# Weights of a quantised MoE block laid out with the contracted dimension on the partitions, and the engine orders laid anew

## The chip, the core and the metric

The kernel runs on one core of a Trainium2 chip. The core has a matrix engine (TensorE, PE in the rows; PEld is its weight load), a vector engine (VectorE, DVE), a scalar engine (ScalarE, ACT), GpSimd (POOL) and a queue engine (SyncE, SP). Each engine works through its own list in order and waits on semaphores for the others. The metric is the device time of one execution in microseconds (us); lower is better.

## What is computed

Four batches of 256 tokens, 256 wide, pass two stages. The first is a small gated MLP whose two linears are quantised to 8 bits per row after a per-column smoothing. The second routes every token to one of 8 experts (at most 128 tokens per expert) and runs the expert's two-layer MLP on it.

```python
def _smooth_quant_linear(x, w):
    amax_x = jnp.max(jnp.abs(x), axis=0)
    amax_w = jnp.max(jnp.abs(w), axis=0)
    s = jnp.sqrt(jnp.maximum(amax_x, EPS) / jnp.maximum(amax_w, EPS))
    xs = x / s
    ws = w * s
    # per-row scales, rounding to 8-bit integers, then
    return x_q @ w_q.T * x_scale * w_scale.T

def _expert_forward(xe, guw, dw):          # first stage, per batch
    h = _smooth_quant_linear(xe, guw)      # guw = fside_BxS2xS2_0[b]: 256 x 256
    gate, up = jnp.split(h, 2, axis=-1)
    return _smooth_quant_linear(jax.nn.silu(gate) * up, dw)   # dw = ctx_1024[b]: 256 x 128
...
x = x + jnp.tanh(g_xattn[0]) * first_stage(_layernorm(x))
x = x + jnp.tanh(g_ffn[0]) * top1_experts(_layernorm(x), w_gate, w1, w2)   # 8 experts, 256 -> 1024 -> 256, gelu
```

The maxima over the rows of a weight (axis 0) are what the smoothing needs; with the contracted dimension on the partitions they are maxima along a row of the memory.

## The kernel before

Everything is held in SBUF; the order of every engine is written out by hand as a list of calls, one list per engine, with batches 0 to 3 (`b`) interleaved. A semaphore ties each call to its producers.

**First stage, per batch b.** SP loads x and the gate/up weight `cw` (L230 to L243), then the router weight `wg`, the down weight `dw`, the two gate scalars, a clear of the scratch rows in HBM, and the expert weights (L244 to L278). VectorE takes mean and variance (`stats1`), GpSimd the reciprocal deviation (`rstd1`), ScalarE the normalised rows (`norm1`; GpSimd for b = 3). TensorE turns the normalised rows (`turn1`) and the weight (`turn1w`) into one PSUM pair `bk[b]`; VectorE takes both maxima (`amax1w`, `amax1`) and their ratio, GpSimd the square root (`root_1`), ScalarE scales both (`scale1`; VectorE for the weight of b = 3), TensorE turns them back (`turn2`), VectorE finds the row scales (`scales1`), ScalarE multiplies and rounds (`quantise1`), GpSimd finishes the rounding (`round1`), TensorE turns the integers (`turn3`) and multiplies (`product1`). `rows1` puts the token scales in a row and the router's logits beside it in `bk[b]`; ScalarE moves that row (`move_row1`). Then `gate_up` on VectorE, `silu` on ScalarE, `act_product` on GpSimd.

The down linear repeats this: `down_turn` turns `dw` on TensorE, `down_amax` takes its maxima on VectorE (and, in its last instruction, scales the logits into `lx`), `amax2`, `root_2`, `scale2`, `turn4`, `scales2`, `quantise2`, `round2`, `turn5`, `move2`, `product2`. `fill` calls are matmuls whose result is not used.

**Routing.** `choose` (VectorE) picks the expert of each token, `expert_out` adds the first stage's result to x, `positions` (TensorE) counts places, `place` and `slot_onehot` make slot numbers and one-hot rows, `square2` and `rstd2` the second norm. `dispatch` (TensorE) gathers the rows of experts 0 and 1 by a product with the one-hot rows, eight matmuls per batch, accumulating over all four batches; `scatter` (GpSimd) writes all rows to the scratch in HBM, two indirect transfers per batch, from which experts 2 to 7 are read back (L281 to L284) once all eight have landed.

**Experts.** For e = 0 to 7: `hidden` (w1), gelu on ScalarE twice (high part and full), `split_high`/`split_low` cut w2 in two parts, `hidden_low` the hidden layer, `expert_out` on TensorE. VectorE enters this stage only after the last scatter has been issued (`scatters_begun`, L932).

## Time and profile before

| | us |
|---|---|
| median of 3 runs | 116.8 (116.26 to 116.91) |
| the profiled execution's own time | 117.76 |
| its span, first to last instruction | 116.0 |
| TensorE busy / VectorE / ScalarE / GpSimd | 98.6 / 86.7 / 72.3 / 56.0 |
| granted TensorE clock, mean | 0.995 |

The span begins with the first instruction and ends with the last; the execution's own time has 1.76 us around it. A row of a timeline gives start, duration, engine, line, operation, tiles and how many instructions were merged; in brackets stands how long the engine had been idle and who ended that. The word `issue` means a wait that the profile ties to nothing.

### The profile page before, as it was taken

To read this page: it belongs to the slowest core of one execution; us is meant where nothing else is said; L and a number is where in the kernel's file an instruction comes from. 1 tells how busy PE (TensorE), PEld (TensorE's weight loads), DVE (VectorE), ACT (ScalarE), POOL (GpSimd) and SP (SyncE) were. 2 spreads that over 40 slices of the span, in tenths; PEclk is the share of its full clock that TensorE was granted. 3 is DMA by queue.
4 is the path that set the end of the run, shared out by engine and by line. 5 is a ranking of instruction groups with operands and counts; after the bars stand their busy time and mean duration, and the time that the engine had idled before them with its cause. 6 is when DMAs were issued, how large, how long until landed. Compare 5 with 4: busy or idle time off the path is not lost.

```text
span 116.0 us, 2229 instructions
## 1 busy us (share of the span) xinstructions
PE 98.6 (85%) x741; PEld 84.4 (73%) x741; DVE 86.7 (75%) x231; ACT 72.3 (62%) x154; POOL 56.0 (48%) x119
## 2 busy tenths in 40 slices
PE   0948868997986898996889999999999999999930
PEld 0227546996845667874689989899999989899820
DVE  6646897999997889682318698999898696939450
ACT  4073579798797899966018564998573739376000
POOL 7855598787969849878670000426030303011041
PEclk9999999999999999999999999999999999999998
DMA  3899998999990942409932999989898860101011
GB/s 108 255 353 291 240 172 291 323 363 353 378 328 26 292 149 94 160 25 237 346 103 66 292 398 353 309 214 408 303 330 280 298 236 10 45 0 51 0 45 45
DMA packets 16218, 24.86 MB, mean 214 GB/s; under 512 B 1368, under 2 KB 13913, under 8 KB 15184
## 3 DMA queue, kind: packets, MB, share of 16 engines
q1 hardware_dynamic: 15440, 22.65, 62.1%
q0 software_dynamic: 768, 2.08, 4.8%
q8 instruction: 6, 0.10, 0.3%
q14 instruction: 4, 0.03, 0.1%
HBM read 20.50 MB, written 4.28 MB: 214 GB/s over the span
## 4 chain that ended last, share of the span: by engine, by line
PE 50%; POOL 16%; DVE 14%; issue 6%; DMA 6%; SPq 2%; ACT 2%; POOLq 1%
PE bk L1182 25%; PE bk L1194 11%; PE bk L1196 6%; DMA cw<-in_ctx_gu 6%; POOL slot_rows L426 4%; POOL row L412 2%; DVE am L740 2%; PE bk L1168 2%; POOL sc L370 2%; DVE am L786 2%; PE bk L1155 2%; PE bk L1208 2%; PE bk L1019 1%; SPq L231 1%; DVE am L721 1%
## 5 line engine op out<-in xcount | busy, mean ns | idle before, releaser
L494 POOL DMA_INDIRECT out<-scrow,gr x8 | 9.5, 1182 | 43.1 <-DVE scrow L961 41.7
L1182 PE MATMUL bk<-rows_w,w_sb 128*128 128x128 f32 x192 | 23.0, 275 | 0.5 <-ACT rows_w L583 0.5
L1182 PEld LDWEIGHTS bk<-rows_w,w_sb 128*128 128x128 f32 x192 | 22.2, 192 | 0.8 <-ACT rows_w L583 0.7
L1194 PE MATMUL bk<-w2p,hh 128*128 128x512 f32 x56 | 20.3, 403 | 0.0
L862 DVE TENSOR_TENSOR w2p<-w_sb,w2p 128x1024 fp32r<-128x1024 f32 x12 | 14.1, 1217 | 3.8 <-POOL begun L482 2.7
L1196 PE MATMUL bk<-w2p,hl 128*128 128x256 f32 x56 | 15.6, 278 | 0.0
L597 ACT ACTIVATE w2p<-w_sb 128x1024 fp32r<-128x1024 f32 x12 | 12.0, 1054 | 5.3 <-PE bk L1196 5.3
L661 ACT ACTIVATE hh<-bk 128x512 fp32r<-128x512 f32 x16 | 9.5, 595 | 4.7 <-PE bk L1182 4.7
L1194 PEld LDWEIGHTS bk<-w2p,hh 128*128 128x128 f32 x56 | 10.5, 188 | 2.1
L1196 PEld LDWEIGHTS bk<-w2p,hl 128*128 128x128 f32 x56 | 10.5, 188 | 0.0
L874 DVE TENSOR_TENSOR hl<-wide_a,hh 128x512 fp32r<-128x512 f32 x16 | 10.4, 683 | 0.0
L1013 PE MATMUL bk<-identb,upper 128*128 128x512 bf16 x25 | 7.8, 438 | 3.0 <-POOL upper L308 3.0
L426 POOL DMA_INDIRECT slot_rows<-row,slot x8 | 8.7, 1090 | 2.9 <-issue 2.9
L663 ACT ACTIVATE wide_a<-bk 128x512 f32<-128x512 f32 x16 | 9.6, 598 | 0.0
L1155 PE MATMUL bk<-row,wide_b 128*128 128x258 f32 x32 | 7.9, 391 | 1.8 <-POOL row L415 1.8
L1155 PEld LDWEIGHTS bk<-row,wide_b 128*128 128x128 f32 x32 | 5.8, 190 | 2.9 <-issue 2.2
L531 ACT ACTIVATE wide_a<-bk,sc 128x256 f32<-128x256 f32 x14 | 5.4, 482 | 2.3 <-POOL sc L370 2.3
L513 ACT ACTIVATE rows_w<-x,sh,rs 128x256 f32<-128x256 f32 x6 | 3.3, 593 | 5.3 <-POOL sh L333 5.3
L540 ACT ACTIVATE wide_b<-bk,q1r 128x256 f32<-128x256 f32 x16 | 6.4, 494 | 0.0
L1013 PEld LDWEIGHTS bk<-identb,upper 128*128 128x128 bf16 x25 | 2.5, 107 | 5.0 <-POOL upper L308 3.0
L1048 PE MATMUL bk<-ident,wide_a 128*128 128x128 f32 x32 | 4.5, 281 | 1.0 <-ACT wide_a L531 0.9
L1048 PEld LDWEIGHTS bk<-ident,wide_a 128*128 128x128 f32 x32 | 3.4, 140 | 2.5 <-ACT wide_a L531 2.4
(164 smaller groups left out, 229.9 us busy)
## 6 DMA issues: line engine op xcount, KB each, us to landing
w_sb<-in_w SPq DMA_DIRECT2D x12, 1024.0 KB, 7.4
slot_rows<-empty SPq DMA_DIRECT2D x1, 1068.0 KB, 9.9
x<-in_x SPq DMA_DIRECT2D x4, 256.0 KB, 4.3
cw<-in_ctx_gu SPq DMA_DIRECT2D x4, 256.0 KB, 6.3
cw<-in_w SPq DMA_DIRECT2D x1, 1024.0 KB, 7.1
out<-row SPq DMA_DIRECT2D x4, 256.0 KB, 2.6
x<-in_w SPq DMA_DIRECT2D x1, 1024.0 KB, 5.8
wide_a<-in_w SPq DMA_DIRECT2D x1, 1024.0 KB, 6.7
```

The lines of the kernel that those rows point to most:

```text
L426: nc.gpsimd.indirect_dma_start(scratch, bass.IndirectOffsetOnAxis(ap=slot[:, b, j:j + 1], axis=0), row[:, b, j, 0:ROW], None, bounds_check ...
L494: nc.gpsimd.indirect_dma_start(out_rows, bass.IndirectOffsetOnAxis(ap=gr[:, e, TOKEN:TOKEN + 1].bitcast(I32), axis=0), yo[:, e % 2, :], No ...
L597: last = nc.scalar.activation(w2p[:, e % 2, n:n + NF // 2, 0], w2v[:, n:n + NF // 2], ACT.Copy)
L661: nc.scalar.activation(hh[:, e % 2, part].rearrange("p n c -> p (n c)"), HB[e % 2][:, m, :], ACT.Gelu_apprx_tanh).then_inc(hhigh_ready, 1)
L663: nc.scalar.activation(hs[:, e % 2, part].rearrange("p n c -> p (n c)"), HB[e % 2][:, m, :], ACT.Gelu_apprx_tanh).then_inc(gelu_ready, 1)
L862: last = nc.vector.tensor_tensor(w2p[:, e % 2, part, 1], w2v[:, part], w2p[:, e % 2, part, 0].bitcast(F32), ALU.subtract)
L874: nc.vector.tensor_tensor(hl[:, e % 2, part], hs[:, e % 2, part], hh[:, e % 2, part].bitcast(F32), ALU.subtract).then_inc(hlow_ready, 1)
L1013: nc.tensor.matmul(bk[b][:, a, :], upper[:], identb[:].unsqueeze(1).to_broadcast([P, 4, P]), start=True, stop=True)
L1155: ins = nc.tensor.matmul(XD[e], hot[:, b, j, e * C:(e + 1) * C], row[:, b, j, 0:RSTD + 1], start=(b == 0 and j == 0), stop=(b == B - 1 and ...
L1182: ins = nc.tensor.matmul(HB[e % 2][:, m, n * C:(n + 1) * C], wv[:, k, o:o + P], xgT[:, e % B, k], start=(k == 0), stop=(k == K - 1))
L1194: nc.tensor.matmul(YB[e % 2], hh[:, e % 2, n], w2p[:, e % 2, n].rearrange("p a d -> p (a d)"), start=(n == 0), stop=False)
L1196: ins = nc.tensor.matmul(YB[e % 2][:, 0:D], hl[:, e % 2, n], w2p[:, e % 2, n, 0], start=False, stop=(n == NF - 1))
```

## The change

`kernel()` on the host reorders four inputs before they are handed over, so that each load is one contiguous row per partition: `cw` becomes [128, K, 256] with the contracted dimension on the partitions, `dw` [128, B, 256], `wg` [128, K, 8], and w2 [E, 128, 8, 256]. What follows from it:

- `turn1w` and `down_turn` are gone from TensorE. `amax1w` reads `cw` in SBUF and also takes the floor and the reciprocal there; `amax1` keeps one reduction and one combined instruction. `down_amax` is gone: one call `down_maxima` reduces all four batches in one reduction over 1024 columns, a floor and a reciprocal; its last instruction lives on as `lx_scale(b)`.
- ScalarE's `scale1(b, 1)` and the second half of `scale2` read SBUF where they read PSUM. `scale1(3, 1)` moves from VectorE to ScalarE, `move_row1` from ScalarE to VectorE.
- The loads of `wg` and of the two gate scalars are issued by ScalarE ahead of its first table load, no longer by SP. SP's order is x, cw alternating for b = 0 to 3, then `dw`. SP waits for the last `scale1` of the weights, not for `turn1`, before it loads w2 of expert 3 over `cw`.
- `slot_onehot(3)` is cut in two instructions, and `dispatch(3)` waits for each apart.
- The lists of all four compute engines are written anew.

```diff
             def load_cw(b):
-                sp.dma_start(cw[:, b], ctx_in[b].rearrange("(j p) d -> p j d", p=P)).then_inc(cw_here[b], 16)
-            load_x(0)
-            load_x(1)
-            load_cw(0)
-            load_x(2)
-            load_cw(1)
...
-            sp.dma_start(dw[:], down_in.rearrange("b (k p) i -> p b k i", p=P)).then_inc(dw_here, 16)
...
+                sp.dma_start(cw[:, b], ctx_in[b]).then_inc(cw_here[b], 16)
+
+            for b in range(B):
+                load_x(b)
+                load_cw(b)
+            sp.dma_start(dw[:], down_in).then_inc(dw_here, 16)
...
+            act.dma_start(wg[:], w_gate).then_inc(wg_here, 16)
+            act.dma_start(gates[:, 0:1], g_xattn.partition_broadcast(P)).then_inc(small_here, 16)
+            act.dma_start(gates[:, 1:2], g_ffn.partition_broadcast(P)).then_inc(small_here, 16)
...
             def amax1w(b):
-                dve.wait_ge(t1w_ready, b + 1)
-                mark(nc.vector.tensor_reduce(am1[:, b, K:2 * K], bk[b][:, 1].rearrange("p (k t) -> p k t", k=K),
-                                             AX, ALU.max, apply_absolute_value=True))
+                dve.wait_ge(cw_here[b], 16)
+                link(nc.vector.tensor_reduce(am1[:, b, K:2 * K], cw[:, b], AX, ALU.max, apply_absolute_value=True))
+                link(nc.vector.tensor_scalar(am1[:, b, K:2 * K], am1[:, b, K:2 * K], EPS, None, ALU.max))
+                inverse_written[b] = mark(nc.vector.reciprocal(rw1[:, b], am1[:, b, K:2 * K]))
...
+            def move_row1(b):
+                dve.wait_ge(row1_ready, b + 1)
+                nc.vector.tensor_copy(xrow[:, b], bk[b][:, 1, 0:T]).then_inc(row1_moved, 1)
...
+            def down_maxima():
+                dve.wait_ge(dw_here, 16)
+                link(nc.vector.tensor_reduce(amd[:], dw[:], AX, ALU.max, apply_absolute_value=True))
+                link(nc.vector.tensor_scalar(amd[:], amd[:], EPS, None, ALU.max))
+                down_inverse[0] = mark(nc.vector.reciprocal(rwd[:], amd[:]))
...
@@ VectorE's list, the routing end
-            scales2(2)
-            choose(0)
-            expert_out(0)
-            scales2(3)
...
+            scales2(2)
+            choose(0)
+            scales2(3)
+            expert_out(0)
```

**VectorE around the first `gate_up`.** In the fences bk0 to bk3 are the PSUM pairs of the four batches; the reduction of am2 from bk3 is `scales1(3)`, wide_a from bk0 is `gate_up(0)`. Before:

```order
L745 RECIPROCAL q1r<-q1s 128x4
L732 TENSOR_SCALAR wide_a<-bk3,sc1 128x256 x2
L752 SCALAR_TENSOR_TENSOR wide_a<-bk0,q1s,scrow 128x256 x2
L761 TENSOR_REDUCE amd<-bk0 128x1
L762 TENSOR_SCALAR amd<-amd 128x1
L763 RECIPROCAL rwd<-amd 128x1
L765 TENSOR_TENSOR lx<-bk0,irs 128x2x8
L740 TENSOR_REDUCE am2<-bk3 128x2 x2
```

The same place now:

```order
L724 RECIPROCAL q1r<-q1s 128x4
L729 COPY scrow<-bk0 128x256
L747 TENSOR_REDUCE amd<-dw 128x4
L748 TENSOR_SCALAR amd<-amd 128x4
L749 RECIPROCAL rwd<-amd 128x4
L736 SCALAR_TENSOR_TENSOR wide_a<-bk0,q1s,scrow 128x256 x2
L719 TENSOR_REDUCE am2<-bk3 128x2 x2
```

The copy of the row and the pass over all down weights stand ahead of `gate_up(0)`; the scaling of the last weight and batch 0's own down maxima are gone.

**GpSimd at the end of the routing.** Three instructions (ve2, row, row) are one `rstd2`, two of the DMA rows one `scatter`. Before, from `rstd2(2)` on:

```order
L406 TENSOR_SCALAR ve2<-ve2 128x2
L412 TENSOR_TENSOR row<-ve2,mhalf 128x2
L415 TENSOR_TENSOR row<-row 128x2
L426 DMA slot_rows<-row,slot 1024x267 x2
L406 TENSOR_SCALAR ve2<-ve2 128x2
L412 TENSOR_TENSOR row<-ve2,mhalf 128x2
L415 TENSOR_TENSOR row<-row 128x2
L426 DMA slot_rows<-row,slot 1024x267 x4
L482 MEMSET begun 128x1
```

Now, from `rstd2(2)` on:

```order
L396 TENSOR_SCALAR ve2<-ve2 128x2
L402 TENSOR_TENSOR row<-ve2,mhalf 128x2
L405 TENSOR_TENSOR row<-row 128x2
L396 TENSOR_SCALAR ve2<-ve2 128x2
L402 TENSOR_TENSOR row<-ve2,mhalf 128x2
L405 TENSOR_TENSOR row<-row 128x2
L416 DMA slot_rows<-row,slot 1024x267 x6
L472 MEMSET begun 128x1
```

`rstd2(3)` no longer stands behind `scatter(1)`; six transfers stand behind it where four stood.

**TensorE at the end of the routing.** row and wide_b into bk0 is `dispatch`, wide_b and intsT `product2`, slot_base the first matmul of `positions`. Before:

```order
L1124 MATMUL bk3<-identb,ints 128x128 x2
L1155 MATMUL bk0<-row,wide_b 128x258 x4
L1131 MATMUL bk3<-wide_b,intsT 128x265 x2
L1146 MATMUL bk2<-slot_base,ones 128x8
...
L1155 MATMUL bk0<-row,wide_b 128x258 x4
L1146 MATMUL bk3<-slot_base,ones 128x8
...
L1155 MATMUL bk0<-row,wide_b 128x258 x8
```

The same place now:

```order
L1110 MATMUL bk3<-wide_b,intsT 128x265 x2
L1136 MATMUL bk0<-row,wide_b 128x258 x4
L1125 MATMUL bk2<-slot_base,ones 128x8
...
L1125 MATMUL bk3<-slot_base,ones 128x8
...
L1136 MATMUL bk0<-row,wide_b 128x258 x12
```

`dispatch(0)` moved behind the last `product2`, and `dispatch(1)` behind the last `positions`, so that three dispatches follow each other.

## Rows read from the trace of the kernel before

**Rows 1.** Windows: busy us (instructions) per engine, granted clock, DMA share, GB/s.

```profile
25.00:40.00 15.00, 12.48 (x105) 9.76 (x101) 13.27 (x50) 12.47 (x38) 12.49 (x30) 1.00 0.82 275
58.50:110.30 51.80, 51.77 (x392) 49.02 (x393) 40.38 (x64) 31.50 (x48) 9.57 (x10) 1.00 0.62 206
```

**Rows 2.** Timeline of the first 23 us: loads, VectorE, GpSimd.

```profile
6.29 2.53 SPq L246 DMA_DIRECT2D gates<-in_g_xattn  x1
...
7.95 0.75 DVE L706 BATCH_NORM_STATS2 st<-x 128x6 f32<-128x256 f32 x2 [0.79 <-DMA x<-in_x]
...
8.74 0.66 PE L1019 MATMUL bk<-ident,cw 128*128 128x128 f32 x4 [1.66 <-DMA cw<-in_ctx_gu]
...
14.78 0.16 DVE L725 TENSOR_TENSOR ra<-am,rw 128x2 f32<-128x2 f32 x1
...
18.25 1.09 POOL L340 TENSOR_SCALAR rows_w<-x,rs,sh 128x256 f32<-128x256 f32 x2 [0.18 <-POOL sh L333]
```

**Rows 3.** Groups of instructions: line, engine, tiles, count, busy us, mean ns, idle before.

```profile
L715 DVE TENSOR_REDUCE am<-bk 128x2 f32<-128x512 f32 x4 | 2.7, 687 | 1.9 <-PE bk L1019 1.9
...
L761 DVE TENSOR_REDUCE amd<-bk 128x1 f32<-128x256 f32 x4 | 1.6, 411 | 0.0
...
L763 DVE RECIPROCAL rwd<-amd 128x1 f32<-128x1 f32 x4 | 0.7, 164 | 0.1
...
L547 ACT ACTIVATE scrow<-bk 128x256 f32<-128x256 f32 x4 | 1.6, 393 | 0.7 <-PE bk L1061 0.7
```

**Rows 4.** The same view: the like operation from SBUF and from PSUM.

```profile
L562 ACT ACTIVATE wide_b<-wide_a,sc 128x256 f32<-128x256 f32 x4 | 2.1, 516 | 0.2 <-POOL sc L391 0.2
...
L563 ACT ACTIVATE wide_b<-bk,sc 128x256 f32<-128x256 f32 x4 | 1.9, 476 | 0.0
...
L773 DVE TENSOR_REDUCE ama<-wide_a 128x1 f32<-128x256 f32 x4 | 1.6, 404 | 0.4 <-POOL wide_a L384 0.4
```

**Rows 5.** The chain of work that ended last: start us, us, what.

```profile
22.97 0.85 DVE wide_a L732 x2
23.82 0.83 DVE wide_a L752 x2
...
38.29 1.14 ACT wide_b L570 x4
```

**Rows 6.** Timeline, 25 to 44 us, VectorE.

```profile
25.35 1.28 DVE L740 TENSOR_REDUCE am<-bk 128x2 f32<-128x512 f32 x2
...
31.56 0.68 DVE L786 TENSOR_REDUCE am<-bk 128x4 f32<-128x512 f32 x1
...
38.62 0.36 DVE L819 SCALAR_TENSOR_TENSOR row<-bk,q2g,lx 128x9 f32<-128x9 f32 x2 [0.37 <-PE bk L1131]
...
39.92 0.87 DVE L796 SCALAR_TENSOR_TENSOR row<-bk,q2g,x 128x256 f32<-128x256 f32 x2
...
40.93 0.69 DVE L786 TENSOR_REDUCE am<-bk 128x4 f32<-128x512 f32 x1
```

**Rows 7.** Timeline, 49 to 59 us: the last dispatches and the first expert.

```profile
51.95 2.01 PE L1155 MATMUL bk<-row,wide_b 128*128 128x258 f32 x8
...
52.28 0.69 DVE L845 TENSOR_TENSOR wide_b<-near,slot 128x512 f32<-128x512 int32 x1
...
54.19 0.19 POOL L406 TENSOR_SCALAR ve<-ve 128x2 f32<-128x2 f32 x1
...
55.60 1.98 PE L1155 MATMUL bk<-row,wide_b 128*128 128x258 f32 x8 [1.65 <-POOL row L415]
...
58.53 2.05 PE L1182 MATMUL bk<-rows_w,w_sb 128*128 128x128 f32 x16 [0.47 <-ACT rows_w L583]
```

**Rows 8.** Timeline, 58 to 67 us: last scatters, the rows read back, the first output matmul.

```profile
58.68 0.97 POOL L426 DMA_INDIRECT slot_rows<-row,slot  x1 [0.30 <-issue]
...
59.96 0.97 POOL L426 DMA_INDIRECT slot_rows<-row,slot  x1 [0.30 <-issue]
...
64.60 0.41 DVE L943 TENSOR_SCALAR rows_w<-gr 128x256 f32<-128x256 f32 x1 [1.17 <-DMA gr<-slot_rows]
...
64.93 1.29 DVE L874 TENSOR_TENSOR hl<-wide_a,hh 128x512 fp32r<-128x512 f32 x2
...
66.16 0.48 PE L1194 MATMUL bk<-w2p,hh 128*128 128x512 f32 x1
```

More of the change, by code:

```diff
@@ L160, in gated_smoothquant_moe_kernel @@
                                                       wide_a[:, 2:4].rearrange("p b c -> p (b c)")]
[L161 removed]
+        w2_place = [w2_sb[:, i] for i in range(3)] + [cw[:].rearrange("p b k o -> p (b k o)"),
                                                       wide_b[:, 0:2].rearrange("p b c -> p (b c)")]
@@ L465, in _ @@
             gate_scale(0)
+            root_2(3)
+            round2(1)
             gate_scale(1)
-            round2(1)
-            root_2(3)
+            round2(2)
             gate_scale(2)
-            round2(2)
+            round2(3)
             gate_scale(3)
             rstd2(0)
-            round2(3)
+            rstd2(1)
             scatter(0)
-            rstd2(1)
             rstd2(2)
+            rstd2(3)
             scatter(1)
-            rstd2(3)
             scatter(2)
@@ L637, in _ @@
             move2(0)
+            scale2(3)
             quantise2(2)
-            scale2(3)
             move2(1)
-            square2(0)
             quantise2(3)
             move2(2)
-            split_high(0)
+            square2(0)
             square2(1)
             move2(3)
+            split_high(0)
             square2(2)
+            square2(3)
             split_high(1)
-            square2(3)
             gelu_table()
@@ L844, in slot_onehot @@
                     dve.wait_ge(consts, 8)
-                nc.vector.tensor_tensor(hot[:, b], near[:].unsqueeze(1).to_broadcast([P, J, NEAR * C]),
-                                        slot[:, b].unsqueeze(2).to_broadcast([P, J, NEAR * C]),
-                                        ALU.is_equal).then_inc(hot_ready, 1)
+                parts = [slice(0, NEAR * C)] if b < B - 1 else [slice(e * C, (e + 1) * C) for e in range(NEAR)]
+                for part in parts:
+                    width = part.stop - part.start
+                    nc.vector.tensor_tensor(hot[:, b, :, part], near[:, part].unsqueeze(1).to_broadcast([P, J, width]),
+                                            slot[:, b].unsqueeze(2).to_broadcast([P, J, width]),
+                                            ALU.is_equal).then_inc(hot_ready, 1)
             def near_in(e):
@@ L880, in _ @@
             stats1(0)
+            amax1w(0)
             stats1(1)
-            amax1w(0)
             stats1(2)
@@ L888, in _ @@
             amax1(1)
+            stats1(3)
             amax1(2)
             amax1w(3)
-            stats1(3)
             scales1(0)
@@ L920, in _ @@
             choose(2)
+            place(1)
             expert_out(2)
-            place(1)
+            expert_out(3)
+            choose(3)
             slot_onehot(1)
-            choose(3)
             place(2)
-            expert_out(3)
+            place(3)
             slot_onehot(2)
-            place(3)
             slot_onehot(3)
@@ L1265, in _ @@
             positions(0)
-            fill(3, 1, 2)
+            fill(3, 1, 1)
             product2(2)
+            turn5(3)
             positions(1)
-            turn5(3)
+            fill(1, 0, 1)
+            product2(3)
             dispatch(0)
-            product2(3)
             positions(2)
+            positions(3)
             dispatch(1)
-            positions(3)
             dispatch(2)
```

180 lines of the change are left out of this document (78 added, 102 removed).

## The prediction, made before the changed kernel was run

> **What bounds the kernel now.** I read the windows by stage first, then the chain of work that ended last, then the timeline where the chain changes engine. The windows split the span in two. From 58.5 to 110.3 us TensorE is busy 51.77 of 51.80 us [rows 1]: the expert stage is its own, and the change leaves its matmuls as they are. Before 58.5 us nobody is saturated: from 25 to 40 us VectorE is busy 13.27, ScalarE 12.47, GpSimd 12.49 and TensorE 12.48 of 15 us [rows 1]. The chain there hops from engine to engine [rows 5] through four interleaved batches. So what counts is when the first `hidden` matmul starts, 58.53 us [rows 7], and whether TensorE is held up after that. TensorE's own load in the head, where most of the removed work lies, decides neither.
>
> **What leaves and what comes, as work.** VectorE loses four down maxima, each 0.41 us and two small ones of 0.16, with starting gaps 0.68, so 2.7 us, and the scaling of the last weight, 0.85 [rows 3, 5]. It gains four row copies. No row shows one on VectorE; the same copy on ScalarE is 0.39 and the 256-column reductions from PSUM are 0.41 [rows 3], so 0.42 each, 1.7 in all. It gains one reduction over 1024 columns, which no row shows: 256 columns cost 0.41, 512 cost 0.69 [rows 3], 0.28 more per 256, so 1.24 (bounds: a saving of nothing against four short ones, 1.64, and twice the step from 0.41, 0.96); with the two small ones 1.6. `amax1` and `amax1w` only exchange two small instructions. Net: -2.7 - 0.85 + 1.7 + 1.6, or -0.25 us. ScalarE loses four row moves, 1.6, and gains two scalings of 256 columns, 1.0 [rows 3, 4]. The twelve ScalarE reads that go from PSUM to SBUF cost 40 ns more each (516 against 476 ns), 0.5 in all; VectorE's reads do not differ (404 against 411) [rows 4]. Net for ScalarE: -0.1 us. The engines that are nearly full keep their load. The removed TensorE work was hidden.
>
> The Trainium skill (VectorE: DVE Perf Modes, The TRN2 errata) speaks against this move: an SBUF source pays a fixed extra latency per instruction on trn2, by its table 52 cycles on ScalarE, but 62 fewer on VectorE. The trace agrees for ScalarE and shows a tenth of it for VectorE. By the table VectorE's net would be 0.3 us better.
>
> **The path, step by step.** I walk the new lists with the durations of the rows and the hand-over gaps seen there; each number is an estimate from them, at best good to some tenths.
>
> Loads. The third block of x was the fourth load and landed at 7.95; the fifth load, a `cw` block, at 8.74 [rows 2]. Now x of batch 2 is the fifth, so 8.6 to 8.7 for it. I give nothing for larger rows; bounds: 8.9 (no gain, some jitter), and 6.6, when VectorE would first be free for it. ScalarE's three issues and its table load now run ahead of its first normalisation. SP's dearest issue took 2.53 us, with nine loads queued ahead of it [rows 2]; three of those would make ScalarE ready only near 10 us and cost some 1.2, since VectorE wants the first turned rows at 10.5. ScalarE's queue is empty, so I take issues of a short kind and nothing on the path; the 1.2 stays in the range.
>
> VectorE from there: `stats1(2)` 0.97, `amax1w(1)` 1.05, `amax1(0)` 0.85, `centre_w` 0.1, `amax1w(2)` 1.05, `amax1(1)` 0.85, `stats1(3)` 0.87, `amax1(2)` 0.85: the third ratio at 15.25, against 14.94 [rows 2]. GpSimd carries this to the end of `norm1(3)`, 19.55 against 18.25 + 1.09 = 19.34 [rows 2]. That is **+0.2**.
>
> Turn, `amax1(3)` (now 0.35 shorter) and `scales1(2)` bring VectorE to 22.85 (22.97 before [rows 5]). Then the new order: row copy 0.42, down maxima 1.6, `gate_up(0)` 0.8, against scaling 0.85, `gate_up(0)` 0.83 and down maxima 0.8. `gate_up(0)` starts at 24.9 instead of 23.82, and `scales1(3)` at 25.7 instead of 25.35 [rows 5, 6]. That is **+0.35**; ScalarE, which has the last weight's scaling now (0.8), is not ready for `silu(0)` before 25.9 either, so the late `gate_up(0)` itself costs little.
>
> From here VectorE no longer has three down maxima in its way and gains back: `scales2(0)` at 31.65 against 31.56 [rows 6], **+0.1**. But ScalarE puts `quantise2(0)` ahead of `scale2(1)`, so batch 1 falls back, and the first `product2` ends at 39.7 instead of 38.6. `turn4(3)` stands behind `turn5(1)` in TensorE's list, and that waits for `round2(1)`, which GpSimd now does after `root_2(3)`. The early root thus buys nothing: `scales2(3)` at 41.45 against 40.93 [rows 6], **+0.5**.
>
> After `scales2(3)` (1.1 us) VectorE is never idle: `expert_out(0)` 0.8, `choose(1)` 1.3 (38.62 to 39.92 [rows 6]), `expert_out(1)` 0.8, `place` and `slot_onehot(0)` 0.9, `choose(2)` 1.3, `place(1)` 0.2, two `expert_out` 1.6, `choose(3)` 1.3, `slot_onehot(1)` 0.7, in sum 8.9: 42.55 + 8.9 = 51.45. Only then can `dispatch(1)` start. Three dispatches of 1.98 follow each other [rows 7], the last starts at 55.4; before, it started at 55.60 after TensorE had stood idle 1.65 for `rstd2(3)` behind a scatter [rows 7]. That wait goes, and what is late next is VectorE. The first `hidden` follows 2.93 after the last dispatch began (58.53 - 55.60 [rows 7]): **58.35, -0.2**.
>
> The scatters. `square2(0)` ends near 45.5; then four `rstd2` of 1.27, and eight transfers at 1.28 us (58.68 to 59.96 [rows 8]), with two gaps of some 0.3 to 0.6 before the first of a run: the last ends near 61.65, against 59.96 + 0.97 = 60.93 [rows 8]. Landing, read-back and `expert_in(2)` took from there to 64.60, and the low part of the hidden layer came 1.0 later [rows 8], at 65.6, 0.55 before TensorE used it at 66.16 [rows 8]. Now it comes at 66.3 and TensorE wants it at 65.95: a wait of 0.35. Sum: -0.2 + 0.35 = **+0.15 us** for everything behind. The split one-hot and the earlier expert loads are covered: TensorE reaches those weights well after they landed, as its full window shows [rows 1]. Costs of the end (110.3 on) do not change. The profiled execution would go from 117.76 to 117.9; the same difference on the median of 116.8 gives 116.9.
>
> **Rivals.**
>
> *Faster: the head starts earlier.* If the load of x(2) lands by 7.7, since `cw` is now one row per partition, or if VectorE's new small pairs overlap better than I count, the whole chain, scatters included, shifts by some 0.9: 116.0. For it: each step above hangs on that landing, and VectorE was idle 0.79 just for it [rows 2]. Against: the fourth and fifth loads were only 0.8 apart. At its bound (VectorE free at 6.6, 2.0 earlier) it would be 114.9.
>
> *Slower: TensorE's list holds back `turn4(3)`.* It decides from the point where `scales2(1)` or `round2(1)` is later than 39.4 or so, since `expert_out(0)` now stands behind `scales2(3)` and so do all squares, norms and scatters. A batch-1 chain one ScalarE quantisation later (1.14 [rows 5]) would make it +0.15 + 0.9: 117.8. For it: four engines at more than eight tenths [rows 1] leave little to absorb it. Against: VectorE has 0.5 us less to do there.
>
> *The removed transposes were warming TensorE.* With fewer matmuls early the granted clock could fall from 2.4 to 1.2 GHz. The granted clock is 1.00 in both windows of the rows [rows 1], and after 1.65 us of idleness a dispatch took 1.98, no more than the 2.01 before it [rows 7]. If it happened in the dispatches, each would take up to twice as long, 2 us more each: 120 and above. The Trainium skill (TensorE: Matmul & The Clock Gate, What's actually happening) calls the throttled state the default that activity releases; no row here shows a fall, so it gets 3 in 100.
>
> **How the numbers follow.** Forecast +0.15, within 0.6 us either way by the unseen costs (reduction +-0.3, copies +-0.2, gaps): 0.38. Faster by the early loads or better gaps: 0.34. Slower by the held-back turn: 0.25; by the clock: 0.03. The measurement can tell about 0.5%, 0.6 us. So faster 0.34, same 0.38, slower 0.28. The range for 8 in 10 runs from 115.3 (most of the early case) to 118.1 (the late one with a few tenths).
>
> **What would show it.** In the profile after: landing of x(2) before `stats1(2)` near 8.6; VectorE's first `gate_up` near 24.9; `scales2(3)` near 41.5; no GpSimd wait ahead of the last dispatch, and three dispatches back to back from about 51.5; first `hidden` near 58.3; a wait of some tenths before the first output matmul, released by the low part. I am wrong if ScalarE's issues delay the first normalisation, if the loads land earlier by more than 0.5, or if the scatters end before 61.

## The result: 3.8 us slower, and the profile after

| | before | changed |
|---|---|---|
| median, us | 116.63 (116.26 to 116.91) | 120.44 (119.71 to 121.08) |
| span of the profiled execution | 116.0 | 117.7 |
| own time less span | 1.76 | 2.55 (others 1.71, 2.74, 2.88) |

The ratio is 1.032, 95% interval 1.028 to 1.036. The forecast was 116.9 with a range to 118.1: wrong, and on the optimistic side. After the first output matmul both kernels keep the same pace, so everything in the span has happened by then.

Batches count from 0. The first ratio is the last instruction of `amax1(0)`, the third that of `amax1(2)`; "the mean" is `mean_w` on TensorE, four small products with the router weight, and `centre_w` is the VectorE instruction that reads them. The head is all up to the third ratio, the tail is the routing from the last `product2` on. Timeline of the changed kernel, VectorE's first 16 us:

```profile
5.73 0.69 DVE L702 TENSOR_REDUCE am<-cw 128x2 f32<-128x512 f32 x1 [1.30 <-DMA cw<-in_ctx_gu]
...
6.74 0.73 DVE L691 BATCH_NORM_STATS2 st<-x 128x6 f32<-128x256 f32 x2
...
8.04 0.75 DVE L691 BATCH_NORM_STATS2 st<-x 128x6 f32<-128x256 f32 x2 [0.35 <-DMA x<-in_x]
...
10.60 0.16 DVE L712 SCALAR_TENSOR_TENSOR ra<-am,rw 128x2 f32<-128x2 f32 x1
12.29 0.17 DVE L771 TENSOR_TENSOR wgc<-wg,bk 128x16 f32<-128x16 f32 x1 [1.52 <-PE bk L1057]
...
15.73 0.16 DVE L712 SCALAR_TENSOR_TENSOR ra<-am,rw 128x2 f32<-128x2 f32 x1
```

Against [rows 2] x of batch 2 comes at 8.04 (7.95 before), but the first context waits to 5.73, the statistics of batch 1 stand behind it in VectorE's new list, and behind the first ratio VectorE waits 1.52 for the mean. TensorE in the same kernel:

```profile
7.36 1.12 PE L1024 MATMUL bk<-ident,rows_w 128*128 128x128 f32 x4 [1.62 <-ACT rows_w L506]
8.27 1.06 PE L1011 MATMUL bk<-identb,upper 128*128 128x512 bf16 x2
10.48 1.11 PE L1024 MATMUL bk<-ident,rows_w 128*128 128x128 f32 x4 [1.15 <-ACT rows_w L506]
11.39 0.86 PE L1057 MATMUL bk<-wg,spread 128*128 128x8 f32 x4
...
13.76 2.10 PE L1011 MATMUL bk<-identb,upper 128*128 128x512 bf16 x5
...
16.57 0.59 PE L1011 MATMUL bk<-identb,upper 128*128 128x512 bf16 x2
```

Four turns take 1.12 where they took 0.66 at 8.74 [rows 2], two fills 1.06 where at 16.57 they take 0.59. The mean (11.39) stands behind `turn1(1)` (10.48) in TensorE's list. Further on: `gate_up(0)`, `scales2(3)`, the last scatter, the rows read back, TensorE (answering [rows 5 to 8]):

```profile
25.27 0.87 DVE L736 SCALAR_TENSOR_TENSOR wide_a<-bk,q1s,scrow 128x256 f32<-128x256 f32 x2
...
41.76 0.68 DVE L777 TENSOR_REDUCE am<-bk 128x4 f32<-128x512 f32 x1
...
58.70 2.05 PE L1163 MATMUL bk<-rows_w,w_sb 128*128 128x128 f32 x16 [0.47 <-ACT rows_w L571]
...
62.26 0.98 POOL L416 DMA_INDIRECT slot_rows<-row,slot  x1 [0.30 <-issue]
...
66.72 0.41 DVE L941 TENSOR_SCALAR rows_w<-gr 128x256 f32<-128x256 f32 x1 [0.97 <-DMA gr<-slot_rows]
...
67.19 0.51 PE L1149 MATMUL bk<-ident,rows_w 128*128 128x128 f32 x2 [0.84 <-DVE rows_w L941]
...
67.88 0.47 PE L1175 MATMUL bk<-w2p,hh 128*128 128x512 f32 x1 [0.19 <-DVE hl L868]
```

The first output matmul is 1.72 later than in [rows 8], as much as the span. That leaves 2 us of the 3.8 unexplained by these two profiles.

### The profile page after: what moved, and what is told of

The parts are those of the page before. It is cut to its first block, busy times and chain, and to the rows that moved or that the text cites. A ratio compares the mean times of both kernels' runs of the same rounds, so it can differ in the third digit from the quotient of the medians.

```text
span 117.7 us, 2183 instructions
## 1 busy us (share of the span) xinstructions
PE 99.3 (84%) x718; PEld 84.1 (71%) x718; DVE 86.2 (73%) x225; ACT 72.0 (61%) x152; POOL 56.0 (48%) x119
## 3 DMA queue, kind: packets, MB, share of 16 engines
HBM read 20.50 MB, written 4.28 MB: 211 GB/s over the span
## 4 chain that ended last, share of the span: by engine, by line
PE 43%; POOL 15%; DVE 11%; ACT 9%; issue 9%; DMA 8%; POOLq 1%; SPq 0%; DVEq 0%
PE bk L1163 18%; PE bk L1175 11%; PE bk L1177 6%; POOL slot_rows L416 5%; DMA cw<-in_ctx_gu 4%; POOL row L402 3%; ACT wide_b L558 3%; DMA slot_rows<-row,slot 2%; DVE am L777 2%; DMA gr<-slot_rows 2%; PE bk L1189 2%; PE bk L1024 2%; ACT wide_a L525 1%; POOL rs L320 1%; DVE am L709 1%
## 5 line engine op out<-in xcount | busy, mean ns | idle before, releaser
L1011 PE MATMUL bk<-identb,upper 128*128 128x512 bf16 x26 | 10.1, 512 | 3.0 <-POOL upper L298 3.0
L1175 PEld LDWEIGHTS bk<-w2p,hh 128*128 128x128 f32 x56 | 10.5, 188 | 2.4 <-issue 0.3
L1011 PEld LDWEIGHTS bk<-identb,upper 128*128 128x128 bf16 x26 | 3.2, 129 | 5.5 <-POOL upper L298 3.0
L1024 PEld LDWEIGHTS bk<-ident,rows_w 128*128 128x128 f32 x16 | 2.7, 201 | 5.9 <-ACT rows_w L506 4.6
L1024 PE MATMUL bk<-ident,rows_w 128*128 128x128 f32 x16 | 3.9, 394 | 3.4 <-ACT rows_w L506 2.8
L1110 PE MATMUL bk<-wide_b,intsT 128*128 128x265 f32 x16 | 4.6, 413 | 1.5 <-ACT wide_b L566 1.5
```

Source lines behind the costliest of these rows:

```text
L1011: nc.tensor.matmul(bk[b][:, a, :], upper[:], identb[:].unsqueeze(1).to_broadcast([P, 4, P]), start=True, stop=True)
L1175: nc.tensor.matmul(YB[e % 2], hh[:, e % 2, n], w2p[:, e % 2, n].rearrange("p a d -> p (a d)"), start=(n == 0), stop=False)
```

## The experiments

Times are medians; a ratio is against runs of the kernel before on the same chip.

### The profiled execution of before was not typical

> The kernel before, unchanged, for a second profile: its profiled execution took 117.76 us with a span of 116.0, while seven others took 116.2 to 117.1 with spans of 114.4 to 115.4, all with 1.7 to 1.8 us outside the span. If that execution is not typical, this one has a span of 114.5 to 115.4, and the rows that the forecast was made from are about 1 us late somewhere; which stage that is, is to be read. Rival: the profiled execution is always the longer one, 115.9 to 116.1 again.

Span 114.8, time 116.53. In 94 executions of before from here on the span has a median of 114.9, and five are at 116.0 or more; outside it lie 1.7 to 1.9 us. The changed kernel's four spans are 117.7 to 118.2. So the change costs 3 us of span (medians 117.95 and 114.9), not 1.7, and in three of its four executions 0.8 to 1.1 outside it. Timeline of the second profile, TensorE and VectorE:

```profile
5.79 1.11 PE L1019 MATMUL bk<-ident,cw 128*128 128x128 f32 x4
...
6.70 1.49 PE L1013 MATMUL bk<-identb,upper 128*128 128x512 bf16 x3
...
13.56 0.16 DVE L725 TENSOR_TENSOR ra<-am,rw 128x2 f32<-128x2 f32 x1
...
39.71 0.69 DVE L786 TENSOR_REDUCE am<-bk 128x4 f32<-128x512 f32 x1
...
54.38 1.98 PE L1155 MATMUL bk<-row,wide_b 128*128 128x258 f32 x8 [1.64 <-POOL row L415]
...
64.94 0.48 PE L1194 MATMUL bk<-w2p,hh 128*128 128x512 f32 x1
```

Its third ratio is ready at 13.72, against 14.94 in [rows 2], and everything behind is 1.22 earlier. In [rows 2] TensorE had stood idle 1.66 for a context load; here it did not wait. The first turns, behind the same six fills, took 1.11 here and 0.66 in the first profile:

```profile
5.78 0.66 PE L1019 MATMUL bk<-ident,cw 128*128 128x128 f32 x4
```

### Loads of three small tensors on ScalarE

The same edit was made on both kernels, in opposite directions: off ScalarE in the changed one, onto it in the one before.

```diff
+sp.dma_start(wg[:], w_gate)              # behind dw; the two gates too
-act.dma_start(wg[:], w_gate)             # ahead of ScalarE's table load; the two gates too
```

> The changed kernel with the loads of wg and of the two gates back on SP's list, behind the load of dw, where ScalarE issued them; nothing else differs. Theory 1 (a second list that issues loads costs time outside the span: own time less span is 1.7 to 2.9 us in four executions of the changed kernel, and 1.76 in the profiled one of the kernel before): 118.7 to 119.4 us, the span as it was at 117.6 +- 0.3. Rival (that time is no cost of the queue, and all 3.8 us are in the span or in its scatter): within 0.4 of the changed kernel's 120.4, and a little above if wg comes later than 11.4 us and holds back the matmuls of the mean, which run at 11.39 now.

> The kernel before with one edit of the change alone: the loads of wg and of the two gates are issued by ScalarE ahead of its first activation, and not by SP. Theory 1 (the extra queue costs time outside the span): +1 to +2 us, 117.7 to 118.7, with a span of 116.0 +- 0.3. Rival: 116.6 +- 0.4; a small loss of up to 0.2 in the span if the first norm1 on ScalarE, begun at 7.6 to 7.7 us before, waits for the issues.

The changed kernel stayed at 120.63; the kernel before went to 119.15 (ratio 1.022, 1.018 to 1.027). Its span grew by 2.3 (medians 117.1 and 114.8), and 2.05 us lay outside in place of 1.75. So theory 1, a cost outside the span, gets 0.3 of the 2.6; the rest is in the span. In the changed kernel with the loads on SP three of four executions have 1.77 to 1.82 outside, but spans of 117.9 to 119.4. Statistics of batch 1 came at 6.01:

```profile
6.01 0.75 DVE L706 BATCH_NORM_STATS2 st<-x 128x6 f32<-128x256 f32 x2 [1.48 <-DMA x<-in_x]
```

where the second profile of before has them at 4.28. Windows from 3.6 to 5.2 us (last columns: share of the DMA engines' time, GB/s), of the second profile of before and then of this kernel:

```profile
3.60:5.20 1.60, 1.60 (x6) 0.44 (x3) 1.60 (x8) 0.00 (x0) 1.26 (x6) 1.00 0.75 184
```

```profile
3.60:5.20 1.60, 1.60 (x6) 0.46 (x3) 0.93 (x4) 0.17 (x1) 1.09 (x5) 1.00 0.57 68
```

The changed kernel shows 86 GB/s there, and 271 with the loads back on SP, where the first context came at 4.51 instead of 5.73. Most of the latter's gain was eaten by a wait that grew, for `wg`, which now came behind nine loads (TensorE stood idle 0.57 for it):

```profile
12.06 0.17 DVE L771 TENSOR_TENSOR wgc<-wg,bk 128x16 f32<-128x16 f32 x1 [2.07 <-PE bk L1057]
```

With the loads on SP the first ratio ends at 9.99 in place of 10.76, but `centre_w` begins at 12.06 in place of 12.29. Which of the three loads costs was tried in the kernel before:

> The kernel before with the load of wg alone issued by ScalarE ahead of its first activation; the two gates stay on SP. If the cost comes with the mere second list (its first transfer holds the shared engines), most of the 2.6 us is here: 118.3 to 119.2, and 3.6 to 5.2 us shows 60 to 120 GB/s. If it comes with the number of small pieces (wg is 256 of them in this kernel), about half: 117.5 to 118.2. Rival (wg is harmless, and landing early it spares VectorE's centre_w a wait): 116.3 to 116.8.

> The kernel before with the loads of the two gates alone issued by ScalarE; wg stays on SP. On SP the first of them held the list for 1.6 to 2.5 us at 5.7 to 6.3, ahead of the clearing of scratch and the first weights. If the gates' 256 pieces of 4 bytes are what slows x and cw: 117.5 to 119.2 with 60 to 130 GB/s in 3.6 to 5.2 us. Rival (they are harmless, and SP's list is freed earlier): 116.2 to 116.8.

`wg` alone: 116.34 against 116.81, ratio 0.996 (0.994 to 0.998), a small gain. The gates alone: 118.42, ratio 1.012 (1.007 to 1.018); x of batch 0 then lands 1.4 us late:

```profile
4.78 0.75 DVE L706 BATCH_NORM_STATS2 st<-x 128x6 f32<-128x256 f32 x2 [1.90 <-DMA x<-in_x]
```

(3.39 in the second profile of before), with 112 GB/s from 2.0 to 3.6 us against 314 there. The time was as expected, the place was not: from 3.6 to 5.2 us this kernel moved 186 GB/s, as much as before. It is the gates: two transfers of 128 pieces of 4 bytes. The Trainium skill (DMA: Bandwidth & Descriptors, Why small descriptors are slow (HBM only)) gives a fixed overhead for each small piece on the DMA engines. The share of engine time beside the bytes from 2.0 to 3.6 us, 0.54 for 112 GB/s against 0.91 for 314, agrees in direction; but at 0.54 the engines were far from full, so that overhead alone does not explain the late landing. Why pieces on a second list hold the first one back, and the same pieces on SP, queued behind x and the contexts, do not, no run shows.

### TensorE's rate in the first 16 us

```diff
-fill(3, 0, 6); turn1(0); fill(3, 0, 2); turn1(1); mean_w(); fill(3, 0, 2); turn1(2); fill(3, 0, 5)
+fill(3, 0, 10); turn1(0); fill(3, 0, 6); turn1(1); mean_w(); fill(3, 0, 3); turn1(2); fill(3, 0, 6)
```

> The changed kernel with more fill matmuls in TensorE's first 16 us: 10, 6, 3 and 6 in place of 6, 2, 2 and 5 (ahead of turn1(0), between turn1(0) and turn1(1), behind mean_w, behind turn1(2)), so that its idle stretches there (1.62 us ahead of 7.36, 1.15 ahead of 10.48) hold work. Theory 2 (TensorE is at 1.2 GHz until about 16 us because the turns of the context are gone and leave it idle): turn1(0) takes 0.60 to 0.66 us and not 1.12, turn1(2) 0.60 and not 1.06; the third ratio ends at 15.1 to 15.4 (now 15.89), gate_up(0) begins at 24.5 to 24.9 (25.27), span 117.0 to 117.4 if the tail follows. Rival (the rate there costs nothing: VectorE and the late stats set the head): the turns are short again and the third ratio stays at 15.7 to 15.9, time as it was.

119.08 us, ratio 1.021 (1.017 to 1.026), 1.2 to 1.4 us better, with useless matmuls added. TensorE and VectorE:

```profile
7.43 0.66 PE L1024 MATMUL bk<-ident,rows_w 128*128 128x128 f32 x4 [0.32 <-ACT rows_w L506]
...
11.52 0.17 DVE L771 TENSOR_TENSOR wgc<-wg,bk 128x16 f32<-128x16 f32 x1 [0.70 <-PE bk L1057]
...
14.96 0.16 DVE L712 SCALAR_TENSOR_TENSOR ra<-am,rw 128x2 f32<-128x2 f32 x1
```

The turns are short again and the third ratio 0.77 earlier, as expected. The first ratio ends at 10.81, no earlier than the 10.76 of the changed kernel: all of the 0.77 is the shorter wait for the mean, 0.70 in place of 1.52. Behind it the gain stays 0.7 to 0.8 down to the rows read back. Of the 1.2 to 1.4 us, 0.65 is in the span (medians 117.95 and 117.3); the rest is time outside it, 1.74 to 1.83 in all four executions here. The granted clock column reads 1.00 (2.4 GHz) in these stretches of both kernels, so it does not show what the durations do: a factor of 1.7 for turns and 1.8 for fills, near that between the levels of 2.4 and 1.2 GHz. TensorE had stood idle 1.62 ahead of the long turns at 7.36 and 1.15 ahead of those at 10.48. The idle time just ahead does not decide alone: in [rows 2] the turns behind an idle 1.66 took 0.66. But in all four profiled kernels that keep the changed kernel's fills the third set of turns, at 12.2 to 12.9, still took 1.06, and in all nine with more fills the second set, at 9.1 to 10.5, took 0.60 to 0.66.

### Both, and the wait for the mean

```diff
 # loads on SP, fills 10, 4, 4, 5; TensorE:
-turn1(1); mean_w(); fill; turn1(2)
+turn1(1); fill; turn1(2); mean_w()
 # VectorE:
-amax1(0); centre_w(); amax1w(2); amax1(1); stats1(3); amax1(2)
+amax1(0); amax1w(2); amax1(1); stats1(3); amax1(2); centre_w()
```

> The changed kernel with three edits in the head: the loads of wg and the gates back on SP behind dw, fills of 10, 4, 4 and 5 in TensorE's first 16 us, and mean_w behind turn1(2) with centre_w behind amax1(2), so that a late wg holds nothing back. Theory (the head is late by three things: ScalarE's loads delay x(1) and cw(0) by 1.2 to 1.9 us, TensorE at 1.2 GHz costs about 0.7, and with the loads on SP the mean's wait of 2.07 us on VectorE ate the gain): third ratio ends at 13.7 to 14.3 (15.89 as changed, 15.12 with the fills alone), span 116.0 to 116.6, time 117.8 to 118.4. Rival (the loads cost nothing in this kernel, as with the loads alone moved, 120.63 against 120.44): third ratio 15.0 to 15.2, time 119.1 +- 0.3 as with the fills alone.

> The changed kernel with the loads of wg and the gates back on SP, mean_w behind turn1(2) and centre_w behind amax1(2), and its own fills of 6, 2, 2, 5, so that TensorE's early rate is left alone. With the fills too the time is 117.44, with the fills alone 119.08, as changed 120.44. If the two costs add up (the loads 1.6, the rate 1.4): 118.7 to 119.1. Rival (the loads' share shows only where TensorE is fast, because at 1.2 GHz its turns hold the chain): 119.5 to 120.3.

With all three: 117.44, ratio 1.0072 (1.004 to 1.010), the third ratio ready at 13.43. Without the fills: 118.41, ratio 1.011 (1.004 to 1.017, six scattered runs), third ratio at 14.16. **The three edits in the head are worth 3.0 of the 3.8 us**, 2.3 in the span (medians 117.95 and 115.65) and 0.7 outside it.

How the 3.0 divides is less sure. By the ratios: fills first 1.2 and the rest 1.6; loads and mean first 2.5 and fills 0.4, with wide intervals. The third ratio moves 0.7 to 0.8 by the fills and 1.7 by the rest in either order, but that is partly luck, as VectorE's rows show. Without the fills, then with all three:

```profile
8.00 0.75 DVE L691 BATCH_NORM_STATS2 st<-x 128x6 f32<-128x256 f32 x2 [0.38 <-DMA x<-in_x]
...
10.56 0.16 DVE L712 SCALAR_TENSOR_TENSOR ra<-am,rw 128x2 f32<-128x2 f32 x1
```

```profile
7.26 0.75 DVE L691 BATCH_NORM_STATS2 st<-x 128x6 f32<-128x256 f32 x2 [0.84 <-DMA x<-in_x]
...
9.84 0.16 DVE L712 SCALAR_TENSOR_TENSOR ra<-am,rw 128x2 f32<-128x2 f32 x1
```

Without the fills the first ratio ends at 10.72, as in the changed kernel, although the loads are back on SP: the 1.7 us at the third ratio is the wait for the mean, 1.52, and `centre_w` itself out of the way. With all three the first ratio ends 0.72 earlier because x of batch 2 came 0.74 earlier, and the fills have no part in that. Over all profiles with the changed order of the loads, `stats1(2)` begins at 6.57 to 8.00 in the ten with the small loads on SP (median 7.26), and at 8.04 to 8.23 in the three with them on ScalarE. So the small loads cost this kernel some 0.8 us in the head by the medians, an estimate, and no execution's landing stands for the others. The mean alone, with the loads left on ScalarE, was never moved: what it would give back by itself is not shown.

### Down maxima in other places

```diff
-scales1(2); move_row1(0); down_maxima(); gate_up(0)
+(a) ... gate_up(0) ... move_row1(1); down_maxima(); amax2(0)
+(b) scales1(1); down_maxima(); amax1(3); ... move_row1(0); gate_up(0)
```

> As the kernel with the three edits in the head, and the down maxima (one reduce of 1.21 us, with its two small operations 1.6 us) moved from ahead of gate_up(0) to behind move_row1(1), where VectorE has amax2(0) next. Theory 4 (they stand on the path that sets gate_up(0)): gate_up(0) begins 1.4 to 1.6 us earlier than without this edit, scales2(0) 0.3 to 1.0 earlier, time -0.3 to -1.0 against the kernel without it. Rival (VectorE is full from 25 to 40 us, 12.42 of 15 us busy, so the work only changes its place): time within 0.3.

> As the kernel with head, tail and scale2 first, and the down maxima moved into VectorE's idle stretch ahead of amax1(3) (1.05 us from 17.74 in the trace of the kernel with the head edits), instead of ahead of gate_up(0). They take 1.6 us, so amax1(3) comes 0.5 to 0.6 later and gate_up(0) 0.9 to 1.1 earlier. Theory 4 in a new form (the down maxima cost what no idle time covers): 0.3 to 1.0 us faster than the kernel without this edit. Rival (the chain of batch 3 behind amax1(3), root_1(3), scale1(3), turn2(3), scales1(3), is as late as gate_up(0)'s, so its delay of 0.5 takes the gain; the other place that was tried, behind move_row1(1), was 1.3 slower): between -0.2 and +0.5.

(a) 118.70, ratio 1.019 (1.010 to 1.028), against 117.44 for the same kernel without it: slower, though `gate_up(0)` began 0.8 earlier, because the maxima now held back `amax2(0)` and `gate_up(1)` (27.73 against 26.76). The profiled execution, 118.05, accounts for 0.6 of this; two of the four took 119.4, and no profile shows why. (b) 117.48 against 116.93 for its base: the maxima sit in an idle stretch of 1.05, delay `amax1(3)` by 0.9 (one small operation took 0.55 there), and what they had cost before `gate_up(0)` returns as a wait of `scales1(3)` for the turns of the last weight:

```profile
24.14 1.29 DVE L719 TENSOR_REDUCE am<-bk 128x2 f32<-128x512 f32 x2 [0.87 <-PE bk L1035]
```

The place that the change chose is the best of three; that theory fell twice.

### The routing tail

First a mistaken form: the orders of before for the tail on all engines, but on GpSimd `round2(3)` left ahead of `rstd2(0)`.

```diff
-rstd2(0); rstd2(1); scatter(0); rstd2(2); rstd2(3); scatter(1)
+rstd2(0); scatter(0); rstd2(1); rstd2(2); scatter(1); rstd2(3)
```

> The changed kernel with the routing tail in the order of the kernel before on GpSimd, VectorE, ScalarE and TensorE (scatter(0) ahead of rstd2(1), scatter(1) ahead of rstd2(3), expert_out(0) ahead of scales2(3), choose, place, square2 and dispatch as they stood); all ahead of that as changed. Theory 3 (the new order of the tail makes the last scatter late, 63.24 against 60.93 us, and that alone carries the 1.7 us by which the first output matmul is late, 67.88 against 66.16): last scatter ends at 61.2 to 61.9, first output matmul at 66.2 to 66.9, time 119.0 to 119.6 (-0.8 to -1.4). Rival (the tail is late because the head is: +0.7 to +0.9 at 20 to 42 us, and the order adds little): last scatter 62.5 to 63.2, time within 0.5 of 120.4.

122.31, ratio 1.050: 1.9 slower, where a gain was expected. `scatter(0)` began at 49.35, no earlier, each return from scatters to arithmetic cost idle time, and TensorE stood still behind it. Timeline and windows:

```profile
53.85 2.89 PE L1136 MATMUL bk<-row,wide_b 128*128 128x258 f32 x8 [2.10 <-POOL row L405]
...
55.00:58.50 3.50, 3.50 (x27) 2.72 (x26) 0.43 (x2) 1.39 (x2) 2.46 (x5) 0.54 1.00 328
```

A dispatch takes 2.89 in place of 2.01 and the granted clock of 55 to 58.5 us is 0.54, near the level of 1.2 GHz; TensorE had stood idle 2.10 ahead of the dispatch. Here the column does show it. Then the whole tail, with `rstd2(0)` ahead of `round2(3)`:

> As the kernel with the edits in the head and the down maxima later, and the whole routing tail of the kernel before on all four engines, GpSimd's from act_product(3) on with it (rstd2(0) ahead of round2(3), which the earlier experiment on the tail lacked; there scatter(0) began at 49.35 against 45.47 us). Theory 3 in its second form (before's tail is better, but only with rstd2(0) and scatter(0) before round2(3) can hold them): scatter(0) begins 45 to 46.5 us, last scatter ends 60.5 to 61.5, time -0.6 to -1.5 against the kernel with the new tail. Rival (the new tail is the better one for this kernel, since each return from scatters to arithmetic on GpSimd costs 0.6 to 0.8 us of idle time): +0.3 to +1.5 against it.

> The changed kernel with the three edits in the head (loads of wg and the gates on SP behind dw; fills of 10, 4, 4, 5; mean_w behind turn1(2), centre_w behind amax1(2)) and the whole routing tail of the kernel before on four engines; the down maxima stay where the change put them. With the head alone 117.44 us; with head, down maxima later and the tail 118.16 against 118.70 without the tail. Theory (the tail of before is worth 0.5 to 1.1 us to this kernel, since scatter(0) begins 1.5 us earlier and the last scatter ends 60.4 against 61.1 to 61.7): 116.4 to 116.9. Rival (the two tails are worth the same, and the difference of the other pair was scatter of the runs): 117.4 +- 0.3.

On top of (a) above it gave 118.16 against 118.70; on the head edits alone 117.46 against 117.44. In those last two the first output matmul begins at 65.86 and 65.83. The tails are worth the same, by different bounds: with the new one TensorE waits 1.06 for the scattered rows; with the old one the rows are there and TensorE's own `dispatch(3)` waits 1.60 for `rstd2(3)`. Two swaps in the middle, on either tail:

```diff
-quantise2(0); scale2(1)        # ScalarE
+scale2(1); quantise2(0)
-act_product(2); root_2(1)      # GpSimd
+root_2(1); act_product(2)
```

> As the kernel with head and tail, and two swaps back to the order of before in the middle: scale2(1) ahead of quantise2(0) on ScalarE, root_2(1) ahead of act_product(2) on GpSimd. In the traces scale2(1) ran 32.27 with the new order and 30.92 us with the old, scales2(1) on VectorE stood waiting 0.55 for its turn, and product2(0) began 36.99 against 36.20. Theory 5 (this order costs the middle 0.6 to 0.8): product2(0) begins 36.1 to 36.4, time -0.4 to -0.8 against the kernel with head and tail, 115.7 to 116.4. Rival (VectorE's list behind it, not this wait, sets scales2(3) and choose(1)): product2(0) moves by the 0.6 and the time by less than 0.2.

> The changed kernel with the three edits in the head and the two swaps in the middle (scale2(1) ahead of quantise2(0), root_2(1) ahead of act_product(2)), with the tail as the change laid it. If the new tail is bound by the scatters and these by the start of scatter(0) behind rstd2(0) and rstd2(1), the swaps' gain of 0.5 to 0.7 at product2(0) must reach scatter(0) to count, and scales2(3) and expert_out(0) come only 0.1 to 0.3 earlier: 117.1 to 117.4 (the old tail with them 116.93). Rival (the tails are worth the same here too): 116.9 +- 0.2.

With the old tail 116.93, ratio 1.001 (0.998 to 1.004): even with before, and 0.5 better than without the swaps. With the new tail 117.70, against 117.44 without the swaps and outside both expectations: nothing gained. There `product2(0)` began 0.26 earlier (36.73), but `scales2(3)` (39.66 against 39.62), which waited 0.46 for its turns, and the first scatter (47.42 against 47.37) did not. TensorE in the former:

```profile
54.51 1.98 PE L1136 MATMUL bk<-row,wide_b 128*128 128x258 f32 x8 [1.60 <-issue]
...
65.07 0.48 PE L1175 MATMUL bk<-w2p,hh 128*128 128x512 f32 x1
```

So one more edit, in this kernel and in the one before:

```diff
-scatter(1); rstd2(3); scatter(2)
+scatter(1, [0]); rstd2(3); scatter(1, [1]); scatter(2)
```

> As the kernel with head, tail of before and scale2 first, and one more edit on GpSimd: the second scatter of batch 1 stands behind rstd2(3) and not ahead of it. In its trace TensorE's dispatch(3) waited 1.60 us for shift2(3) (begun 54.51), the chain of near rows and hidden matmuls behind it ended at 64.91, while the scattered rows were in at 64.1. Account (the old tail is TensorE's bound, by the place of rstd2(3) on GpSimd): dispatch(3) begins 53.1 to 53.4, the last scatter stays at 59.8 to 60.0, the first output matmul begins 64.2 to 64.5 instead of 65.07, time -0.5 to -0.8: 116.1 to 116.5, faster than the kernel before. Rival (the rows' way in is the bound already): first output matmul at 64.9 or later, time within 0.2 of 116.9.

> The kernel before with that one edit on GpSimd alone: the second scatter of batch 1 behind rstd2(3). In its second profile dispatch(3) waited 1.64 us for shift2(3), the first output matmul began at 64.94 and the scattered rows were in at 63.7 (VectorE's L943 at 63.30). Account: first output matmul at 64.0 to 64.3, time -0.6 to -0.9, 115.7 to 116.1. Rival (the scattered rows are the bound already, or square2(3) is not done in time, so that the scatters behind it come late): time within 0.2 of before, or slower by the 0.3 to 1.0 that the later scatters cost.

The kernel before with it: 116.02 against 116.56, ratio 0.995 (0.992 to 0.998), **faster than both kernels**. The changed kernel with all edits: 116.35, ratio 0.998 (0.995 to 1.001), even. TensorE in the former:

```profile
53.31 1.98 PE L1156 MATMUL bk<-row,wide_b 128*128 128x258 f32 x8 [0.36 <-POOL row L415]
...
63.93 0.51 PE L1169 MATMUL bk<-ident,rows_w 128*128 128x128 f32 x2
64.62 0.47 PE L1195 MATMUL bk<-w2p,hh 128*128 128x512 f32 x1 [0.19 <-DVE hl L875]
```

The wait fell from 1.64 to 0.36 and `dispatch(3)` came 1.1 earlier, but the first output matmul only 0.3 (0.5 counted from the third ratio, which was 0.2 late here): the low part, behind the scattered rows, ends last now. The expected 64.0 to 64.3 missed that. In the changed kernel with all edits the first output matmul, at 65.06, had not moved from 65.07, against an expected 64.2 to 64.5; its third ratio came 0.4 later in that execution, which hides a gain of that size.

### w2 alone

> The kernel before with one edit of the change alone: w2 is laid out by kernel() with its contracted dimension on the partitions, so that its load moves runs of 8 KB and not of 1 KB on every partition; all orders as before. Rival theory 6 (the larger runs change the head, since w2(0) shares the queues with nothing that is waited for by then, or the span's outside part): if larger packets crowd out the cw and x loads, +0.2 to +1.0 us; if they help, -0.2 to -0.5. My theory: no difference, 116.5 +- 0.3, with w_sb's median landing 5.9 to 6.5 us after issue in place of 7.4, since no wait of the expert stage ends last on w2.

116.77 against 116.76, ratio 0.998 (0.995 to 1.001); the loads of w_sb landed in 6.2 us, against 7.4 in the first profile of before and 6.5 in the second, so most of that difference is the first profile's own. The larger rows of w2 are worth nothing here. The larger rows of `cw` and `dw`, and the new order of x and `cw`, were not tried apart.

## Why the prediction was wrong, point by point

Read against the second profile of before, the steps fall apart in two groups. Us behind the end of the third ratio:

| | before, second profile | forecast | changed |
|---|---|---|---|
| the third ratio itself | 13.72 | 15.25 | 15.89 |
| `gate_up(0)` | +8.83 | +9.65 | +9.38 |
| `scales2(3)` | +25.99 | +26.20 | +25.87 |
| first `hidden` | +43.58 | +43.10 | +42.81 |
| last scatter ends | +46.00 | +46.40 | +47.35 |
| first output matmul | +51.22 | +51.06 | +51.99 |

- **The step that failed: the wait at `centre_w`, put at nothing.** The walk gives it 0.1 us. Up to the first ratio the changed kernel was 0.77 ahead of the walk (10.76 against 11.53, by the walk's own durations), since x of batch 2 came at 8.04 and not at 8.6; then VectorE stood 1.52 for the mean; from `amax1w(2)` to the third ratio the walk was right again (3.51 against 3.62). The walk followed VectorE alone here, because "TensorE's own load in the head" was said to decide nothing. The mean stands behind `turn1(1)`, and that began at 10.48, where the second profile of before has 9.43: the statistics of batch 1 began at 6.74 in place of 4.28. Two more steps of the prediction stand behind that wait.
- **First, "the removed TensorE work was hidden"**: true as work and false as activity. `turn1(1)` and the mean took 1.11 and 0.86, against 0.60 and 0.51 in the second profile of before, and more fills cut the wait by 0.82. The slow turns were a rival with 3 in 100, placed in the dispatches; they struck in the first 16 us. That the granted clock read 1.00 in the windows was no evidence, as the column does not show it there.
- **Second, the loads.** "ScalarE's queue is empty, so I take issues of a short kind and nothing on the path." The issues were short (0.40, 0.46 and 0.45) and ScalarE was in time. But beside their transfers the first context came 1.2 late (5.73 against 4.51 with the loads on SP), and in the kernel before the same three loads cost 2.6 us. The 1.2 kept in the range was priced for ScalarE's list, not for the transfers. I had costed the DMAs as instructions and not as traffic. (The row behind it, 2.53 for an issue, had ten loads queued ahead, not nine.) Of the 2.46 by which the statistics of batch 1 were late, 1.27 remain with the loads on SP (5.55): that is the new order of the loads and of VectorE's list. Which share of the 3.0 us is the loads' and which the place of the mean, the runs do not separate.
- **The base.** The forecast walked from an execution whose own time, 117.76, stood 1.0 above the median shown. I noted the difference and applied the sum to the median, but the rows of the head carried that excess: 14.94 was 13.72 elsewhere. The third ratio's forecast, 15.25, so looks nearly right against 15.89 while the change really cost 2.2 there and not 0.3. That nearness is luck: a landing forecast too late, from a late profile, offset half of a wait that was not forecast.
- **The middle was right.** The row copy took 0.40 (0.42 forecast), the maxima 1.21 (1.24), and, counted from the third ratio, the walk to `gate_up(0)`, `scales2(3)` and the first `hidden` is within 0.3 of the rows. The swap of `quantise2(0)` and `scale2(1)` makes `choose(0)` 0.8 later behind the third ratio, as the walk had it, and costs nothing behind the new tail.
- **The scatters: a term mis-sized.** 46.40 against 47.35. The power in `rstd2(0)` took 1.21 and not 0.7, the first two transfers 1.26 and 1.28 and not 0.97, and two starts cost 0.78 and 0.58. The rows of before had such transfers and starts too (1.26 at 45.47, 1.54 and a start of 0.58 at 51.30), and the forecast took the short ones for all. So TensorE waited 1.03 (0.84 + 0.19), not 0.35. With the head mended this is what is left: 117.44 against 116.5, with the first output matmul at 65.83 against 64.94.
- **The rivals.** The faster one hung on x of batch 2; it came at 8.04, between the forecast 8.6 and the 7.7 of the rival, and what it bought by the first ratio was lost in the wait for the mean. The slower one, `turn4(3)`, did not happen: `scales2(3)` was 0.3 earlier than forecast, relative to the head.
- **Outside the span.** Taken as unchanged, it is 0.8 to 1.1 of the 3.8 us in three of four executions. It was 2.5 to 2.9 us in these three, and in four of fourteen of the three other kernels with the fills of 6, 2, 2, 5; never in 82 with more fills or in any of before. The two go together; what the time outside the span is, and why, stays open.

## What to carry to other kernels

A transfer has two prices: the list that issues it, and the engines that carry it; a tiny broadcast moved to an idle list can delay the large load that everything waits for. An instruction of 0.1 us can still hold a list for 1.5: when a list is walked, ask at each step what its inputs wait for on the other engines. When turns are removed from TensorE, ask what their activity was paying for, and compare the duration of a like instruction, not only the clock column. Before a sum is built on one profile, set its own time against the median: an excess of 1 us sits in some row, and a second profile tells which.

## What the runs showed of the hardware

- Two loads of 128 pieces of 4 bytes each, issued on ScalarE's list while SP's held the large loads, cost the kernel before 1.6 us: from 2.0 to 3.6 us the DMA engines moved 112 GB/s in place of 314, and x of batch 0 landed 1.4 late. With the two on SP, behind the large loads, it did not.
- `wg` alone on ScalarE's list (8 KB in 256 pieces) was a gain of 0.4 us.
- TensorE's turns of four took 1.01 to 1.12 or 0.60 to 0.66 us, nearly all of them, with a granted clock of 1.00 in both. More fills ahead of and between them made them short; yet the same program, behind the same six fills, had them at 0.66 in one execution and at 1.11 in another. In one kernel, behind an idle time of 2.10 us, the granted clock read 0.54 and a dispatch took 2.89 in place of 2.01.
- A 1024-column reduction from SBUF took 1.21 us on VectorE, a 256-column copy from PSUM 0.40.
- GpSimd's power on 128x2 took 1.12 to 1.21 in place of 0.70 in each of five kernels in which VectorE's wide comparison of `slot_onehot` had begun just before it (45.86 and 45.91 in the changed kernel). That the one causes the other was not tried.
- Loads of x with the same lists ahead of them let `stats1(2)` begin anywhere from 6.57 to 8.00 us in ten profiles.
